# Attention on one core: queries and keys projected with channels on partitions, rope by a second projection of swapped channels, 64-row operands laid out by DMA

## The reference

```python
Q, K, V = (proj(Wq, bq), proj(Wk, bk), proj(Wv, bv))     # 16 heads of 16 channels
cos, sin = _rope_cache(s)
Q = _apply_rope(Q, cos, sin)                              # even, odd channels of a head rotated
K = _apply_rope(K, cos, sin)
scores = jnp.einsum('bhqd,bhkd->bhqk', Q, K) * (1.0 / math.sqrt(D_K))
scores = jnp.where(causal[None, None], scores, -jnp.inf)
probs = jax.nn.softmax(scores, axis=-1)
att = jnp.einsum('bhqk,bhkd->bhqd', probs, V)
return jnp.einsum('bsd,ed->bse', att.transpose(0, 2, 1, 3).reshape(b, s, d), Wo) + bo
```

## Time and profile before

| | us |
|---|---|
| median of three runs | 1029.8 (1029.27, 1029.8, 1035.34) |
| the profiled execution | 1032.82, of which its span is 1031.6 |
| attention, from the last L1484 to the last L1597 | 73.65 to 363.64 of the span |
| PE busy, DVE busy, ACT busy, POOL busy over the span | 750.4, 638.6, 390.6, 315.8 |
| mean granted clock of PE | 0.855 |

### The profile page before, as it was taken

One profiled execution on the slowest core, in us unless ns is written; L12 is line 12 of the kernel. 1 busy time (PEld: TensorE's weight loads), 2 busy tenths in 40 slices (PEclk: granted clock), 3 DMA queues, 4 the chain that ended last, 5 costly groups with the idle time before them and its releaser, 6 DMA issues. The chain is left out here.

```text
span 1031.6 us, 11267 instructions
## 1 busy us (share of the span) xinstructions
PE 750.4 (73%) x3818; PEld 542.1 (53%) x3818; DVE 638.6 (62%) x1069; ACT 390.6 (38%) x784; POOL 315.8 (31%) x373
## 2 busy tenths in 40 slices
PE   2965887668889778859906836869958888776980
PEld 1755655545455466758705524535535455565870
DVE  4977465665666167635435737588967999762333
ACT  3313344213655423203303563846543555121330
POOL 2242124200111130150060014537835677224006
PEclk9988599866999979589956959979969999968995
DMA  4600000000000060045430000000042000003434
GB/s 171 199 1 0 1 1 1 1 1 1 1 1 1 1 245 5 33 149 162 148 97 6 0 1 0 1 1 0 1 161 84 0 1 1 28 24 123 131 125 122
DMA packets 27816, 52.36 MB, mean 51 GB/s; under 512 B 2288, under 2 KB 22128, under 8 KB 26608
## 3 DMA queue, kind: packets, MB, share of 16 engines
q1 hardware_dynamic: 24688, 43.25, 12.0%
q0 software_dynamic: 3072, 8.39, 2.7%
HBM read 34.20 MB, written 17.43 MB: 50 GB/s over the span
## 5 line engine op out<-in xcount | busy, mean ns | idle before, releaser
L1155 PE MATMUL PS<-FB,C 128*128 128x512 f32 x256 | 132.3, 616 | 1.2 <-DVE FB L1831 1.2
L1266 ACT ACTIVATE FA<-PS 128x512 f32<-128x512 f32 (+3 forms) x192 | 82.7, 497 | 63.1 <-PE PS L930 62.1
L1913 POOL TENSOR_SCALAR_AFFINE_SELECT FA<-FA 128x128 f32<-128x128 f32 x128 | 36.9, 298 | 192.2 <-ACT FA L1266 190.6
L1950 POOL TENSOR_TENSOR FB<-FB,RBF 128x512 f32<-128x512 f32 x51 | 65.7, 1289 | 70.6 <-DVE FB L1822 70.6
L432 PE MATMUL PS<-C,FB 128*128 128x128 f32 x250 | 45.8, 308 | 56.7 <-DVE FB L1463 37.4
L905 PE MATMUL PS<-RA 128*128 128x128 f32 (+3 forms) x288 | 79.1, 398 | 4.5 <-DVE FA L1560 1.5
L930 PE MATMUL PS<-RA 128*128 128x512 f32 (+3 forms) x192 | 66.6, 408 | 17.1 <-ACT FA L1266 8.0
L432 PEld LDWEIGHTS PS<-C,FB 128*128 128x128 f32 x250 | 36.3, 160 | 69.6 <-DVE FB L1463 38.5
L1931 POOL DMA_INDIRECT FB<-GY,FB x32 | 30.8, 963 | 135.3 <-DMA GY<-FB 126.3
L905 PEld LDWEIGHTS PS<-RA 128*128 128x128 f32 x288 | 55.6, 239 | 31.2 <-DVE FA L1558 13.2
L1053 PE MATMUL PS<-WE,FB 128*128 x248 | 62.4, 396 | 0.0
(11 more groups left out here) (269 smaller groups left out, 1765.1 us busy)
## 6 DMA issues: line engine op xcount, KB each, us to landing
FB<-GX SPq DMA_DIRECT2D x14, 512.0 KB, 4.7
GY<-FB SPq DMA_DIRECT2D x14, 512.0 KB, 3.1
WE<-in_wr SPq DMA_DIRECT2D x4, 1536.0 KB, 11.4
WE<-in_wr SPq DMA_DIRECT2D x3, 2048.0 KB, 13.0
GX<-FA SPq DMA_DIRECT2D x1, 3968.0 KB, 13.9
FA<-in_w SPq DMA_DIRECT2D x2, 1024.0 KB, 7.6
FB<-in_we SPq DMA_DIRECT2D x4, 384.0 KB, 3.4
X<-in_x SPq DMA_DIRECT2D x2, 512.0 KB, 8.4
```

Source lines behind the costliest of these rows:

```text
L1155: pe.matmul(bank(m), ident, shc[k % 4], start=n == 0, stop=n == DN - 1).then_inc(*yad.inc(ch, n, m))
L1266: act.activation(PT[n % 16][:, c0:], bank(4 + ring_no[(x, *a)] % 3)[:, c0:], ACT.Exp, scale=0.25).then_inc(*exd.inc(*a))
L1913: pool.affine_select(out=dd, in_=dd, compare_op=ALU.is_ge, fill=0.0, base=0, pattern=[[1, P]], channel_multiplier=-1).then_inc(*sel.inc(*a))
L1950: pool.tensor_tensor(shc[k % 4], sh[k % 5], Cs[(stc.no[ch, n] - 1) % 2], ALU.mult).then_inc(*cma.inc(ch, n, m))
```

## The change

Q and K are now projected with channels on partitions and 512 tokens along the free axis, in two halves `u` of eight heads each: step `pj` for (q or k, u). Each has two products: the channels as they are, and the same channels with even and odd swapped. Rope is then (product + bias) times cosine, (swapped product + bias) times sine, each one DVE instruction on 128x512 (`rp1`), a sum on POOL, a high copy on ACT and a low one on DVE (`rp2`). The host puts the channels in an order in which 64 partitions hold 16 channels of four heads, and six DMAs of SP lay each result out in KT or QT, where two heads share the partitions: rows 0 to 63 and rows 64 to 127. `keys` and both `turn`s are gone. Scores are now matmuls on 64 rows, and the mask is four matmuls of 64 rows instead of two of 128. The maximum is 8 rows of 512: four small transposes (`mtt`), one ACT copy, two DMAs. The padding rows of KT are set by POOL in the step `wo`, those of QT by DMA from there. The exponentials have 12 buffers instead of 16. Projection of the second chunk is spread over the heads of the first, and the first group's maxima of the second chunk stand beside the last heads of the first. Semaphores of late steps are shared (`gat`, `wl`), and the weights of the experts come in four loads instead of three the second time.

In the cut diff below the parts of the engines' programs stand in this order: SP (`rp2`, `mtt`), PE (`pj`, `mtt`, the scores), ACT (`wq`), DVE (`wq`, `wo`, `rp1`, `rp2`), POOL (`wo`).

```diff
-def project_steps(ch):
-    if ch:
-        yield from norm_steps(1, 1)
-    yield [("xbo", ch)]
-    for i in range(TC):
-        yield [("proj", ch, i)]
-        yield [("rope1", ch, i)]
-        yield [("rope2", ch, i)]
-        if i:
-            yield [("keys", ch, i - 1)]
-    yield [("keys", ch, TC - 1)]
+def project_steps(ch, what):
+    n = len(what)
+    for k in range(n + 2):
+        seg = []
+        if 2 <= k:
+            seg += [("rp2", ch, *what[k - 2])]
+        if 1 <= k <= n:
+            seg += [("rp1", ch, *what[k - 1])]
+        if k < n:
+            seg += [("pj", ch, *what[k])]
+        yield seg
...
 def attention_steps():
-    yield from project_steps(0)
+    q0, q1, k0, k1 = ("q", 0), ("q", 1), ("k", 0), ("k", 1)
+    yield [("xbo", 0), ("mzero", 0, 0)]
+    yield from project_steps(0, [q0, k0, q1, k1])
+    yield from values_steps(0)
     yield from maxima_steps(0, 0)
-    for g in range(3):
-        yield from weave((maxima_steps(0, g + 1), 0.6), (heads_steps(0, g), 1))
-    yield from weave((chain(heads_steps(0, 3), output_steps(0)), 1), (chain(project_steps(1), maxima_steps(1, 0)), 0.8))
+    yield from weave((chain(maxima_steps(0, 1), norm_steps(1, 1), [[("xbo", 1)]]), 1), (heads_steps(0, 0), 1))
+    yield from weave((chain(maxima_steps(0, 2), project_steps(1, [k0, k1]), values_steps(1)), 1), (heads_steps(0, 1), 1))
+    yield from weave((chain(maxima_steps(0, 3), project_steps(1, [q0])), 0.7), (heads_steps(0, 2), 1))
+    yield from weave((chain(heads_steps(0, 3), project_steps(1, [q1]), output_steps(0)), 1), (maxima_steps(1, 0), 0.8))
...
+                elif x == "rp2":
+                    ch, w, u = a
+                    hi, lo = stage[(rpl.no[ch, w, u] - 1) % 2]
+                    to = QT[:, 4 * u:4 * u + 4, :] if w == "q" else KT[:, 4 * u:4 * u + 4, ch * CH:ch * CH + CH]
...
+                    for src, at in ((hi, 0), (hi if w == "k" else lo, 16), (lo if w == "k" else hi, 48)):
+                        for r in range(2):
+                            sp.dma_start(to[64 * r + at:64 * r + at + 16, :, :].bitcast(F), src[64 * r:64 * r + 64, :].bitcast(F)).then_inc(plc[w, u].sem, 16)
+                elif x == "mtt":
+                    ch, g = a
+                    sp.wait_ge(*mtc.at(ch, g))
...
+                elif x == "pj":
...
+                    for v in range(2):
+                        c0 = (("q", "k").index(w) * 4 + v * 2 + u) * P
+                        t = group(bk[:, v, :], [q for k in range(2) for q in three([y[:, k, c0:c0 + P] for y in Wq], xn(k, ch))])
+                    t.then_inc(*pjd.inc(*a))
...
+                elif x == "mtt":
+                    ch, g = a
+                    bk = claim_pair(x, *a)
+                    pe.wait_ge(*mxd.at(ch, g))
+                    for i in range(TC):
+                        t = turn_over(bk[0:8, 0, i * P:i * P + P], Mhl[:, i, :].bitcast(F))
+                    t.then_inc(*mtr.inc(ch, g))
...
                     def score(out, ii, hh, c0, c1, start, stop):
-                        return pe.matmul(out, QT[:, 4 * (g % 2) + hh, ii * P:ii * P + P], KT[:, 2 * g + hh // 2, c0:c1], start=start, stop=stop)
+                        r = slice(64 * (hh % 2), 64 * (hh % 2) + 64)
+                        return pe.matmul(out, QT[r, 2 * g + hh // 2, ii * P:ii * P + P], KT[r, 2 * g + hh // 2, c0:c1], start=start, stop=stop, skip_group_check=True)
...
+                elif x == "wq":
+                    act.wait_ge(*qld.at())
+                    act.activation(Wall[0], wst, ACT.Copy).then_inc(*awh.inc())
...
                 elif x == "wq":
-                    dve.wait_ge(*qld.at())
-                    split(Wq[0].rearrange("p k n -> p (k n)"), Wq[1].rearrange("p k n -> p (k n)"), wst[0]).then_inc(*awq.inc("q"))
-                elif x == "wo":
-                    dve.wait_ge(*old.at())
-                    split(Wo[0].rearrange("p k n -> p (k n)"), Wo[1].rearrange("p k n -> p (k n)"), wst[1][:, 0:512]).then_inc(*awq.inc("o"))
+                    dve.wait_ge(*awh.at())
+                    dve.tensor_tensor(Wall[1], wst, Wall[0].bitcast(F), ALU.subtract).then_inc(*awq.inc())
+                elif x == "rp1":
...
+                    for v, t in enumerate((t1, t2)):
+                        c0 = ("q", "k").index(w) * 4 + v * 2 + u
+                        last = dve.scalar_tensor_tensor(t, bk[:, v, :], bqk[:, c0:c0 + 1], rope[v][:, ch * CH:ch * CH + CH], ALU.add, ALU.mult)
+                    last.then_inc(*rpt.inc(*a))
+                elif x == "rp2":
+                    k = rpl.no[tuple(a)] - 1
+                    hi, lo = stage[k % 2]
+                    dve.wait_ge(*rph.at(*a))
+                    dve.tensor_tensor(lo, sets[k % 2][2], hi.bitcast(F), ALU.subtract).then_inc(*rpl.inc(*a))
...
                 elif x == "wo":
                     pool.wait_ge(*wq.at(1))
                     vv = V.rearrange("p t (h c) -> p (t h) c", c=32)
-                    pool.memset(QT.bitcast(F), 0.0)
-                    pool.memset(vv[:, :, 16:17], 1.0)
-                    pool.memset(vv[:, :, 17:32], 0.0)
+                    pool.memset(vv[:, :, 16:17], 1.0).then_inc(*p_own.inc())
+                    pool.wait_ge(*p_own.at())
+                    pool.memset(vv[:, :, 17:32], 0.0).then_inc(*vset.inc())
+                    pool.wait_ge(*vset.at())
+                    for r in (32, 96):
+                        pool.memset(KT[r:r + 16, :, :].bitcast(F), 0.0).then_inc(*p_own.inc())
+                        pool.wait_ge(*p_own.at())
+                    for r in (32, 96):
+                        last = pool.memset(KT[r:r + 2, :, :].bitcast(F), -1.0)
+                        last.then_inc(*(p_own if r == 32 else kset).inc())
+                        pool.wait_ge(*(p_own if r == 32 else kset).at())
```

458 lines of the change are left out of this document (203 added, 255 removed).

## The result

The changed kernel took 1047.45 us (median of four runs, 1046.5 to 1054.82) where the kernel before took 1032.57 beside it: 1.0158 times as long, 95% interval 1.009 to 1.022. The forecast was 993 in a range of 968 to 1020, so the sign was wrong. The table by stages of the profiled run (span 1044.9, granted clock 0.816 where it was 0.855) answers to the earlier trace rows; the stages are projection, first maxima, heads of groups 0, 1, 2 and 3 of the first chunk, groups 0 to 2 of the second, and its last heads with the output.

What follows compares the result with a forecast made beforehand. No single engine was taken to bound the kernel: a chain across engines in the projection, PE in the second chunk's groups. Terms 9.8 - 4.5 + 1.4 - 4.0 - 33 - 6.7 + 0 = -37.0 gave 993 us, range 968 to 1020.

Steps and rivals of the forecast that it cites:

- Term 1: Feed-forward half ahead of the attention: four new memsets of 7.0 us hold VectorE's casts, last sum into X +9.8 us later.
- rival C: Feed-forward half: casts find no gap between the memsets, +24 instead of +9.8 us, 1007 us in all; chance 0.12.
- Term 5: First chunk's group 1 to the second chunk's first heads: spread projection overlaps, 72.3 us instead of 105.0, -33 us.
- the bound of 90: Same stretch, 90 us instead of 72 if the overlap is not had; as a rival 1011 us in all, chance 0.13.
- term 6: Second chunk, groups 0 to 2, PE bound: transposes go, small ones and mask products come, -6.7 us, bounds -2 and -19.
- A: Score products: pairs of heads run together on the two halves of the array, about 973 us in all; chance 0.17.
- E: Score and mask products: a 64-row product costs more than a 128-row one, mainly in the second chunk, 1049 us; chance 0.07.
- Terms 2, 3, 4 and 6: Projection -4.5 us; first maxima +1.4; heads of group 0 -4.0; second chunk's groups 0 to 2 -6.7.
- Term 7: Last heads and output of the second chunk: no change, 0 us.

Runs made afterwards that it cites:

- e1: Changed kernel with KT's padding made by two short memsets of 1024 values and two DMAs instead of four memsets of 8192; 0.991 of the kernel before.
- e2: Kernel before with four more GpSimd memsets of 8192 values on 16 partitions, each followed by a wait for its end; 1.023 of the kernel before.
- e3: Changed kernel with all score products on 128 rows instead of 64 and the mask as two products of 128 rows (another computation); 0.999 of the kernel before.
- e10: Changed kernel with one product of each three in the second chunk's projections of Q and K (less exact); 1.000 of the kernel before.
- e4: Changed kernel with padding by DMA, the second chunk's projection and values reordered, and the first chunk's output woven into the second's first heads; 0.993 of the kernel before.
- e13: Changed kernel with three of the second chunk's four Q and K projections cut into four pieces of three products each; 1.019 of the kernel before.
- e8: Changed kernel with padding by DMA, the second chunk's work and first output reordered, and all score and mask products on 128 rows (another computation); 0.976 of the kernel before.
- e14: Changed kernel with padding by DMA and three of the second chunk's Q and K projections cut into pieces of three products; 0.996 of the kernel before.
- e5: Changed kernel with the order of the kernel before, the second chunk's projection beside the first chunk's last heads and output; 1.010 of the kernel before.
- e12: Changed kernel with padding by DMA and the order of the kernel before, its projection not spread over the heads; 0.991 of the kernel before.
- e15: Changed kernel with padding by DMA, projections in pieces, and the four DMAs of each high part issued before the wait for the low part; 0.991 of the kernel before.
- e9: Changed kernel with all score and mask products on rows 0 to 63, both heads of a pair alike (another computation); 1.072 of the kernel before.

## Why the prediction was wrong

**Term 1** had the mechanism and half its size. "A cast on VectorE does not run beside a memset" was right and so were four times 7.0 us. The step that failed is "Followed": only casts were made to wait, and the two `tensor_scalar` of the normalisation, which stand between them on DVE, do not occur in it, so they cost nothing. They took 13.38 us beside two memsets instead of 0.73. +21.0 came for +9.8; e1 has -4.7 without the memsets, so that these cost 25.7 at this point, and 24 to 25 us of the time by the ratios of e1 and e2. Its rival C had nearly the size (+24), for another reason.

**Term 5** is the larger miss, 31 us, and failed at "This is where the change bears": TensorE's work was priced at the full clock ("about that at full clock", "0.22" for 512 columns), and the bound of 90 was tied to a clock near 0.6, for which 0.13 was given. The clock was 0.64 and the stretch 103: 28.1 and 24.9 us in groups 1 and 2 for 21.8 and 16.5, and 50.2 for 30 in the last stage (with 4 for rope's waits beside them). The work itself was priced well. In the last stage DVE was to be busy 23 us and was 23.37; TensorE was to be busy 21.6 at the full clock and was 36.28 at 0.57, which is 20.7 at the full one (though 19.4 at 0.57, one of its terms, is 11 and not 9.7). Over the whole stretch TensorE was busy 76.75 of 104.99 us before and 78.24 of 103.19 after, as a window of each shows:

```profile
136.69:241.68 104.99, 76.75 (x440) 54.84 (x441) 66.53 (x106) 33.35 (x75) 23.24 (x56) 0.83 0.00 1
```

```profile
154.06:257.25 103.19, 78.24 (x393) 50.24 (x391) 45.82 (x68) 24.12 (x56) 19.38 (x52) 0.64 0.23 32
```

With each stage's busy time times its clock that is 64 and 50 us at the full clock, an estimate from the rows of both kernels: the change took 14 us of work off TensorE, and the clock, down from 0.83 to 0.64, took them back. TensorE's idle time hardly moved, 28 and 25 us. By the same estimate 50 and 25 would be 75, near the 72 of the forecast.

e3 and e10 bear this out. On 128 rows the stretch took 92.1 us with TensorE busy 67.24, with fewer products 92.8 with 65.88: 25 and 27 us idle as before, and what is won, 11 and 10 us, is TensorE's busy time. What keeps the clock from being full in the rest of it (0.83 in e3) is not shown: no run took the idle time away. The output that stands alone and the placement waits are real, but e4 and e13 show no time won by moving or cutting work.

**The 64 rows** were a side remark in term 6 and two rivals. A was right that pairs run together and wrong that this makes the kernel faster. E had the sign, 64-row products costing more in sum, and the wrong place for it: no product is slower at a given clock, the clock is lower. No part of the prediction had that mechanism. Its cost is 17 us (e3). Where the clock was nearly had all the same, in the three groups of e10 at 0.96, the pairs took 78.7 us, against e3's 80.0 at 1.00.

**Terms 2, 3, 4 and 6.** The projection won 1.9, not 4.5, because a set of six DMAs is not hidden where a stage buffer is needed again ("The six DMAs for each result hide behind it", but ACT waits 5.63 and 5.80 us). The first maxima came out 2.9 better; 2.0 of that are the pairs, as e3, where nothing is paired, takes 15.5 us for them instead of 13.5. In group 0 TensorE's busy time fell by the 3.8 us forecast, from 18.91 to 15.13, and the group kept its 21 us at clock 0.66, so that time was not what it waited for. Term 6 came to -4.4 for -6.7, with TensorE 75 us busy at 0.85 instead of 82 at 0.95: fewer busy microseconds, each worth less. Term 7 lost 1.8 in the same way, 33.0 us at clock 0.76.

**The balance.** Memsets +24 to 25 (e1, e2), 64 rows +17 (e3, and e8 against e4), all else together some -26, by subtraction, where the kernel before has its turns and transposes. Open is what moves the clock in stages whose instructions are the same: the three groups took 78.7 us at 0.96 in e10, 83.4 at 0.89 in e1, 86.3 at 0.85 in the changed kernel and in e14, 89.7 at 0.79 in e5 and 93.3 at 0.74 in e12. Differences of 5 us between the variants with 64 rows are within that.

**The best versions that compute the same** are e1, e12 and e15, 0.991 of the kernel before; e4 with 0.993 is no different. e8 shows 0.976 for 128-row products; to compute the same it would need the other head's rows of Q at zero, 8192 values a partition instead of 4096, where about 1000 are free. That wasn't tried.

## What to carry to other kernels

A memset on GpSimd cost what its values per partition cost (3.51 us for 4096 on 128 partitions, 7.0 for 8192 on 16 or on 2), and while it ran VectorE could neither cast nor scale in SBUF, though a subtraction kept its 0.69 us: copy a short padding on with DMAs, or set it where VectorE is idle. Two concurrent halves in place of 128 rows made the products 1.6 times as fast and still lost, both where engines wait for each other (103.2 us against 92.1) and where TensorE is the bound (86.3 against 80.0): read the granted clock after such a split before counting its gain. A gain that is argued from overlap needs its durations at the clock that the overlapped stage will have, and where that is unknown the pessimistic end belongs in the forecast, not in a rival.

## What the runs showed of the hardware that was not expected

- The granted clock was lower with products on 64 rows than on 128, at more busy time: 0.61 at 115.64 us busy of 117.37 on the same 64 rows (e9), 1.00 at 74.30 of 79.98 on 128 (e3), and 0.74 to 0.96 on alternating halves.
- Products of 64 rows on alternating halves ran 1.6 times as fast as 128-row ones at either clock (0.75 against 1.19 us for eight, 1.31 against 2.16); on the same 64 rows they took as long as on 128.
- An fp32 `tensor_scalar` from SBUF to SBUF was held by a GpSimd memset like a cast (13.38 us for two beside two memsets; 0.73 for two without).
- A DMA of 128 KB inside SBUF, 64 partitions to 16 of 4x512 values, took about 0.6 us to issue on SP (six in 3.81) and landed after 5.6 us (median of 48), more than the 512 KB ones of the earlier trace rows with their 3.1.
